# A graph network on one core: scores one tile later at the second norm, and a bias copied into PSUM in place of ten bias matmuls

## Chip, cores and metric

The kernel runs on one core of one Trainium2 chip. The metric is the device time of one execution in microseconds (us). TensorE does the matmuls, VectorE and ScalarE elementwise work and evictions of PSUM, GpSimd (POOL) set-up work and indirect DMAs, SyncE (SP) most plain DMAs.

## Reference, cut to what matters

N = 1250 nodes of D = 512 numbers, 21250 edges. Two blocks, each with a norm in front and a residual behind:

```
h = max(layernorm(x), 0)                              # first norm
hw = h @ W0 + b_w                                     # the product, with W0's bias
e = leaky_relu((hw @ a1)[dst] + (hw @ a2)[src] + b_a)
x = x + segment_sum(softmax_over_dst(e) * hw[src])
h = max(layernorm(x), 0)                              # second norm
gates = softmax(h @ gate_W + gate_b)                  # scores of 4 experts, the best 2 are taken
agg = segment_sum(h[src], dst) / degree               # neighbour sums
x = x + sum over the 2 best experts of gate * sage2(sage1(agg, h))
```

## The kernel before

Nodes are held as T = 10 tiles of P = 125 rows. Float32 products are made of three float32r matmuls each: every operand is split into a high part (a copy, made by ScalarE) and a low part (whole minus high, made by VectorE). Order between the engines is written out by hand with semaphores; each engine runs its own list in order.

**First stage, ten batches** (`tile_and_batch(b)` on TensorE, L1702 on). A batch counts edges of 125 nodes and makes the product of one tile. TensorE: turn the normed tile (4 transposes, L1716); 25 count matmuls into banks 0 to 4 (L1692), each set of five waiting for one-hots of VectorE and for the eviction of its bank; 8 matmuls of 4 columns into bank 7 (L1740, L1743), called the columns below, which wait for `hT_lo`; then the product into bank 6: a bias matmul (L1754, ones times a two-row form of the bias) and twelve matmuls (L1756 to L1758). VectorE, in each batch: loads of registers from `tab_b`, 25 one-hots (L1197), the low part of the product of the batch before (`product_low`, L1177), the low part of the turned tile (`turned_low0`, L1181). ScalarE: high part of the product (`product_high`), high part of the turned tile, five `column` instructions, the next normed row (`norm`, L756), the eviction of the five count banks (`windows_out`). Before the batches come the hot blocks (`hot_block`, L1650), with small table matmuls between them. Behind the last batch `spread` (L1700) spreads a row of source sums made by `spread_out` (L1230), which the attention weights need.

**Attention**, then the **second norm**, one loop over tiles on TensorE: `turn2` (transposes, L1828, banks 6 and 7), `neighbours1(t, 0)` (ten matmuls, L1867 and L1868, which add tile t to five neighbour sums), `logits` (8 matmuls of 8 columns, L1837 and L1838). The turned tile is evicted as high part `h2T_hi` (ScalarE) and low part `h2T_lo` (VectorE, L1389); `logits` need both. The sums of tiles 0 and 1 read `nat_a` (low part L1361), those of tile t >= 2 `nat_hi` and `nat_lo` (`rows_low`, L1378), and each the counts `CT_hi` (`counts_high`, L1356). On VectorE `attended(QN - 1)` ends the attention; behind it stand the statistics of the last two tiles, `inv_deg`, and a loop over tiles:

```python
for t in range(T):
    if t >= 2:
        rows_low(t)
    if t == 3:
        scaled(1, late)
    if t + 2 < T:
        counts_high(t + 2)
    dve.wait_ge(*h2T_hi_ready(t + 1))
    v.tensor_tensor(h2T_lo[:, :, t * P:(t + 1) * P], ...
```

The rest (two layers of four experts, then routed tiles) is not touched.

Of the kernel before, what the change touches and what calls it, by code (L numbers as in the profile page):

```python
# [14 lines left out]
F32 = mybir.dt.float32  # L15
# [22 lines left out]
def gnn_kernel(nc, x, src, dst, W0, b_w, a_vec, b_a, gate_W, gate_b, Wl, bl, Wr, out):  # L38
# [37 lines left out]
    with ctx:  # L76
# [4 lines left out]
        def at(name, shape, dt, offset):  # L81
            return nc.alloc_sbuf_tensor_at(name, shape, dt, offset=origin + offset)
# [64 lines left out]
        q_at = at("q_at", [2 * CR + 1, CR], F32, 22432)  # L147
        q_sel = at("q_sel", [2 * CR + 1, CR, P], F32R, R1 + 20480)
        a_b = at("a_b", [128, 2, D], F32, R1)
        bw_b = at("bw_b", [P, D], F32, R1 + 4096)  # L150
        spill = [at(f"spill_{k}", [128, D], F32, R1 + 6144 + 2048 * k) for k in range(2)]
        g_b = at("g_b", [NW, NCH], F32, 28704)
        g_hit = at("g_hit", [NW, NCH], F32, 29408)
# [43 lines left out]
        s_part = early("s_part", [P, T, 2], F32)  # L197
        s_both = early("s_both", [P, T, 2], F32)
        spark = early("spark", [1, 1], F32)
        bw_2 = early("bw_2", [128, D], F32R)  # L200
        ones_2 = early("ones_2", [128, P], F32R)
        column = early("column", [P, 2 * BW, G], F32)
        diag = early("diag", [P, 8, P], F32)
        assert o4[0] <= R5 + 12032
# [107 lines left out]
        def signals(names, start=0):  # L312
            return [Signal(ctx.enter_context(nc.semaphore(n)), start) for n in names.split()]
# [39 lines left out]

        (w0_hi_ready, w0_lo_ready, wa_f_ready, ab_ready, wa_ready,
         var_ready, std_ready, norm_ready, h_ready, turned, hT_hi_ready, hT_lo_ready, s_done, hw_done,
         hw_hi_ready, hw_lo_ready, bw_hi_ready, bw_lo_ready, sums_used, small_ready, s_ready, sd_ready, sd_spread, row_ready) = signals(
             "w0_hi_ready w0_lo_ready wa_f_ready ab_ready wa_ready "
             "var_ready std_ready norm_ready h_ready turned hT_hi_ready hT_lo_ready s_done hw_done "
             "hw_hi_ready hw_lo_ready bw_hi_ready bw_lo_ready sums_used small_ready s_ready sd_ready sd_spread row_ready")

        (low_ready, zl_ready, ze_ready, pf_ready, ph_ready, pl_ready, p_used, summed, den_done, rden_ready, x2_ready,
         stats_ready) = signals(
# [54 lines left out]
        def f32(ap):  # L417
            return ap.bitcast(F32)
# [145 lines left out]
        def _(pool):  # L564
# [39 lines left out]
            g.tensor_copy(wbase[:], wbase_i[:])  # L604
            g.memset(tab_x[:], 0).then_inc(consts.sem, 1)
            g.memset(tab_b[:], 0).then_inc(consts.sem, 1)
            link(g.memset(f32(bw_2[:]), 0.0))
            link(g.memset(f32(ones_2[:]), 1.0))
            pool.wait_ge(*small_in(48))
            link(g.tensor_copy(bw_2[0:1, :], bw_b[0:1, :]))  # L610
            g.tensor_tensor(bw_2[32:33, :], bw_b[0:1, :], f32(bw_2[0:1, :]), ALU.subtract).then_inc(bw_lo_ready.sem, 1)
            beyond = counts_beyond(pool)
            with pool.If(beyond):
                for q in range(QN):
# [96 lines left out]
        def _(act):  # L711
# [51 lines left out]
            def turned_high0(b):  # L763
# [2 lines left out]
                    act.wait_ge(*hw_done(b))  # L766
                copy(hT_hi[:], ps[:, 5, 0:KC * P].rearrange("p (c n) -> p c n", n=P)).then_inc(hT_hi_ready.sem, 1)

            def windows_out(b):
                act.wait_ge(*batch_done(b + 1))  # L770
                for k in range(BW):
                    copy(CT[:, :, (b * BW + k) * W:(b * BW + k + 1) * W], ps[0:P, k, 0:WT].rearrange(
                        "p (i t) -> p t i", t=T)).then_inc(window_out.sem, 1)
# [18 lines left out]
            for b in range(T):  # L792
                if b > 0:
                    product_high(b - 1)
                turned_high0(b)
                if b + 1 < T:
                    columns(b + 1)
                    norm(b + 1)
                else:
                    act.wait_ge(*spark_ready(2))  # L800
                    a.activation(spark[:], spark[:], ACT.Exp)
                windows_out(b)

            beyond = counts_beyond(act)
# [230 lines left out]
        def _(dve):  # L1035
# [328 lines left out]
            for t in range(2):  # L1364
                counts_high(t)
                first_low(t)
            attended(QN - 1)
            dve.wait_ge(*stats_ready(T))
            normed(1, late)
            dve.wait_ge(*gw_hi_ready(1))  # L1370
# [10 lines left out]
# [4 lines that stand above are left out]
                    scaled(1, late)  # L1385
                if t + 2 < T:
                    counts_high(t + 2)
                dve.wait_ge(*h2T_hi_ready(t + 1))
                v.tensor_tensor(h2T_lo[:, :, t * P:(t + 1) * P], ps[:, 6 + t % 2, 0:KC * P].rearrange(  # L1389
                    "p (c n) -> p c n", n=P), f32(h2T_hi[:, :, t * P:(t + 1) * P]), ALU.subtract  # L1390
                                ).then_inc(h2T_lo_ready.sem, 1)
            for t in range(2):
                rows_low(t)
            dve.wait_ge(*logits_done(T))
# [219 lines left out]
        def _(pe):  # L1614
# [51 lines left out]
            def sum_tables():  # L1666
                pe.wait_ge(*n_ready(1))
                pe.wait_ge(*cols_ready(1))
                mm(ps[0:NW, 7, 0:1], tri[:], tab_f[:, 1:2], start=True, stop=True).then_inc(n_summed.sem, 1)

            def turn_tables():
                pe.wait_ge(*tab_f_ready(1))
                for k in range(3):
                    last = mm(ps[0:1, 7, 4 + k * NW:4 + (k + 1) * NW], tab_f[:, k:k + 1], ident[0:NW, 0:NW], start=True,
                              stop=True)
                last.then_inc(tab_turned.sem, 1)

            for u in range(NU):
                hot_block(u)
                if u == 2:  # L1680
                    spread_spans()
                if u == 3:
                    turn_edges()
                if u == 7:
                    sum_tables()
                if u == 8:
                    turn_tables()

            def count_step(k, slot, first, opens):

# [12 lines left out]
            def tile_and_batch(b):  # L1703
                if b == 0:
                    pe.wait_ge(*tab_ready(1))
                los = first_chunks(pe, b)
                more = more_here(pe, b)

                if b > 0:
                    pe.wait_ge(*hT_lo_ready(b))  # L1710
                else:
                    pe.wait_ge(*hot_ready(len(HOT_ACT)))
                    pe.wait_ge(*hot_dve_ready(len(HOT_DVE)))
                pe.wait_ge(*h_ready(b + 1))
                for c in range(KC):
                    last = nc.tensor.transpose(ps[:, 5, c * P:(c + 1) * P], h_f[:, c * 128:(c + 1) * 128],  # L1716
                                               ident[0:P, 0:P])
                last.then_inc(turned.sem, 1)

                for k in range(BW):  # L1720

                    pe.wait_ge(*window_out(b * BW, k + 1, BW))

                    pe.wait_ge(*step_ready(b * BW, k + 1))
                    count_step(k, k, los[k], True).then_inc(step_used.sem, 1)
                with pe.If(more):
                    for k in range(BW):
                        def step(first_chunk, before):
                            pe.wait_ge(*more_ready(before, 1))
                            count_step(k, 0, first_chunk, False).then_inc(more_used.sem, 1)  # L1730
                        more_steps(pe, b * BW + k, step)

                pe.wait_ge(*hT_lo_ready(b + 1))
                if b == T - 1:
                    pe.wait_ge(*s_ready(1))
                o = ps[0:P, 7, 4 * b:4 * (b + 1)]
                if b == 0:
                    pe.wait_ge(*wa_ready(2))
                for c in range(KC):
                    first = mm(o, hT_hi[:, c], wa[:, c], start=c == 0, stop=False, skip_group_check=True)  # L1740
                    if c == 0:
                        first.then_inc(batch_done.sem, 1)
                    last = mm(o, hT_lo[:, c], wa[:, c], start=False, stop=c == KC - 1, skip_group_check=True)  # L1743
                last.then_inc(s_done.sem, 1)
                if b == T - 1:
                    spread(0)

                if b > 0:
                    pe.wait_ge(*hw_lo_ready(b))
                else:  # L1750
                    pe.wait_ge(*w0_lo_ready(1))
                    pe.wait_ge(*bw_lo_ready(1))
                o = ps[0:P, 6, :]
                mm(o, ones_2[:], bw_2[:], start=True, stop=False)  # L1754
                for c in range(KC):
                    mm(o, hT_hi[:, c], W0_hi[:, c], start=False, stop=False)  # L1756
                    mm(o, hT_hi[:, c], W0_lo[:, c], start=False, stop=False)  # L1757
                    last = mm(o, hT_lo[:, c], W0_hi[:, c], start=False, stop=c == KC - 1)  # L1758
                last.then_inc(hw_done.sem, 1)

            for b in range(T):
# [122 lines left out]
            for t in range(T):  # L1884
                pe.wait_ge(*(a_lo_ready(t + 1) if t < 2 else h2_lo_ready(t - 1)))
                pe.wait_ge(*ct_hi_ready(t + 1))
                neighbours1(t, 0)
                if t == 0:
                    pe.wait_ge(*gw_lo_ready(1))
                logits(t)  # L1890
                if t + 2 < T:
                    turn2(t + 2)
            pe.wait_ge(*h2_lo_ready(T))
            for t in range(T):
                neighbours1(t, 1)
# [181 lines left out]
```

## Time and profile before

| | |
|---|---|
| median of 3 runs | 783.39 us (781.53 to 783.49) |
| the profiled execution's own time | 783.68 us |
| its span in the trace | 781.6 us |
| mean granted clock of TensorE | 0.986 |
| TensorE busy | 750.2 us, 96% |
| VectorE, ScalarE, GpSimd busy | 395.0, 274.9, 122.8 us |

Times in the trace count from the start of the span. PE is TensorE, DVE VectorE, ACT ScalarE. Matmuls are pipelined, so one's recorded time reaches into the next; the distance from start to start is what a matmul costs in a stream. The granted clock is 1.00 at 2.4 GHz and 0.50 at 1.2 GHz.

### The profile page before, as it was taken

To read this page: it belongs to the slowest core of one execution; us is meant where nothing else is said; L and a number is where in the kernel's file an instruction comes from. 1 tells how busy PE (TensorE), PEld (TensorE's weight loads), DVE (VectorE), ACT (ScalarE), POOL (GpSimd) and SP (SyncE) were. 2 spreads that over 40 slices of the span, in tenths; PEclk is the share of its full clock that TensorE was granted. 3 is DMA by queue.
4 is the path that set the end of the run, shared out by engine and by line. 5 is a ranking of instruction groups with operands and counts; after the bars stand their busy time and mean duration, and the time that the engine had idled before them with its cause. 6 is when DMAs were issued, how large, how long until landed. Compare 5 with 4: busy or idle time off the path is not lost.

```text
span 781.6 us, 11775 instructions
## 1 busy us (share of the span) xinstructions
PE 750.2 (96%) x3755; PEld 610.1 (78%) x3755; DVE 395.0 (51%) x979; ACT 274.9 (35%) x567; POOL 122.8 (16%) x137
## 2 busy tenths in 40 slices
PE   5899999999899999999999999999999999999994
PEld 3589978888788887777777777788887888888883
DVE  8888888997652538622624424333323323323320
ACT  6945575565542521412413313111211211211221
POOL 5000000000000101840000100222322323323211
PEclk9999999999899999999999999999999999999997
DMA  9000001111401247799698781599427954339900
GB/s 219 16 4 4 3 3 34 33 33 49 147 1 55 76 132 239 220 335 341 210 366 292 244 327 60 160 271 335 86 60 193 321 173 88 67 98 262 318 12 7
DMA packets 45320, 115.10 MB, mean 147 GB/s; under 512 B 7300, under 2 KB 7432, under 8 KB 45241
## 3 DMA queue, kind: packets, MB, share of 16 engines
q1 hardware_dynamic: 28581, 77.60, 30.7%
q0 software_dynamic: 8016, 19.59, 10.8%
q10 hardware_dynamic: 8644, 16.86, 6.6%
q8 instruction: 49, 0.80, 0.4%
q14 instruction: 30, 0.25, 0.1%
HBM read 64.85 MB, written 50.07 MB: 147 GB/s over the span
## 4 chain that ended last, share of the span: by engine, by line
PE 91%; DVE 4%; ACT 2%; issue 1%; POOL 0%; DVEq 0%; ACTq 0%; POOLq 0%
PE ps L1622 18%; PE ps L1623 18%; PE ps L1624 18%; PE ps L2008 7%; PE ps L2007 6%; PE ps L1692 3%; PE ps L1867 3%; PE ps L1868 3%; PE ps L1929 2%; PE ps L2018 1%; PE ps L1973 1%; PE ps L1784 1%; PE ps L1756 1%; PE ps L1650 1%; PE ps L1758 1%; PE ps L1757 1%
## 5 line engine op out<-in xcount | busy, mean ns | idle before, releaser
L2008 PE MATMUL ps<-slots,CTs 125*128 x230 | 91.0, 396 | 0.0
L2007 PE MATMUL ps<-slots,CTs 125*128 x207 | 81.6, 394 | 0.0
L1453 DVE TENSOR_TENSOR he_t<-ps,b_b 125x512 f32<-125x512 f32 x40 | 27.5, 690 | 105.8 <-PE ps L1624 72.6
L962 ACT ACTIVATE slots<-he_t 125x512 fp32r<-125x512 f32 x40 | 25.4, 635 | 150.9 <-DVE he_t L1453 136.0
L1546 DVE CAST CTs<-ps 125x512 fp32r<-125x512 f16 (+1 forms) x69 | 37.2, 595 | 76.5 <-PE ps L1929 72.9
L678 POOL DMA_INDIRECT out<-tg,rec x23 | 37.3, 1620 | 182.2 <-ACT tg L1012 143.3
L1622 PE MATMUL ps<-W,agT_hi 128*125 128x512 f32 x160 | 63.5, 397 | 0.0
L1622 PE MATMUL ps<-W,h2T_hi 128*125 128x512 f32 x160 | 63.4, 396 | 0.0
L1624 PE MATMUL ps<-W,agT_lo 128*125 128x512 f32 x160 | 63.3, 396 | 0.0
L1623 PE MATMUL ps<-W,agT_hi 128*125 128x512 f32 x160 | 63.2, 395 | 0.0
L1623 PE MATMUL ps<-W,h2T_hi 128*125 128x512 f32 x160 | 63.2, 395 | 0.0
L1624 PE MATMUL ps<-W,h2T_lo 128*125 128x512 f32 x160 | 63.1, 394 | 0.0
L1592 DVE TENSOR_TENSOR tm<-ps,b_b 128x512 f32<-128x512 f32 x23 | 15.9, 692 | 82.0 <-PE ps L1624 82.0
L1197 DVE TENSOR_SCALAR onehot_g<-iota_h,column 125x250 bf16<-125x250 f16 x250 | 49.7, 282 | 8.3 <-PE ps L1692 7.0
L1005 ACT ACTIVATE heT<-ps 128x512 fp32r<-128x512 f32 x23 | 13.7, 598 | 107.3 <-PE ps L1973 102.9
L2008 PEld LDWEIGHTS ps<-slots,CTs 125*128 125x128 f32 x230 | 43.3, 188 | 9.6
L2007 PEld LDWEIGHTS ps<-slots,CTs 125*128 125x128 f32 x207 | 38.9, 188 | 9.0
L1622 PE MATMUL ps<-nat_hi,p_hi 125*125 125x512 f32 x100 | 42.4, 424 | 2.2 <-issue 1.8
L1016 ACT ACTIVATE agn<-ps,rec 128x512 f32<-128x512 f32 x23 | 15.8, 687 | 79.4 <-PE ps L2008 75.9
L1622 PE MATMUL ps<-slots,heT 128*128 x92 | 40.0, 435 | 0.0
L1623 PE MATMUL ps<-nat_lo,p_hi 125*125 125x512 f32 x100 | 39.6, 396 | 0.0
L1624 PE MATMUL ps<-nat_hi,p_lo 125*125 125x512 f32 x100 | 39.5, 395 | 0.0
(302 smaller groups left out, 1675.6 us busy)
## 6 DMA issues: line engine op xcount, KB each, us to landing
he_d<-slots SPq DMA_DIRECT2D x30, 448.0 KB
slots<-he_d SPq DMA_DIRECT2D x30, 448.0 KB
w_d<-slots SPq DMA_DIRECT2D x3, 4096.0 KB, 19.6
slots<-w_d SPq DMA_DIRECT2D x24, 512.0 KB
t_d<-he_t SPq DMA_DIRECT2D x40, 224.0 KB
raw<-in_L_gnn_Wl ACTq DMA_DIRECT2D x4, 1024.0 KB, 9.6
raw<-in_L_gnn_Wr ACTq DMA_DIRECT2D x4, 1024.0 KB, 5.7
slots<-in_L_gnn_Wl ACTq DMA_DIRECT2D x4, 1024.0 KB, 9.8
```

The costliest lines, as they stand in the source:

```text
L678: g.indirect_dma_start(out, bass.IndirectOffsetOnAxis(ap=i32(rec[:, i, 2:3]), axis=0), tg[i % 3][:], None, bounds_check=N - 1, oob_is_err= ...
L962: a.activation(HE[:, t, 0:D], he_t[:, (x * T + t) % 4, :], ACT.Relu).then_inc(he_hi_ready.sem, 1)
L1197: last = v.tensor_scalar(onehot_g[:, k, j, :], iota_h[:], column[:, b % 2 * BW + k, j:j + 1], None, ALU.is_equal)
L1453: v.tensor_tensor(he_t[:, n % 4, :], ps[0:P, bank_of(x, g, t), :], b1_b[:, x % 2, :], ALU.add).then_inc(pre_ready.sem, 1)
L1546: v.tensor_copy(CTs[:, 4 * r:4 * r + n, :], turned_counts(r, n)).then_inc(cts_ready.sem, 1)
L1622: mm(o, l_hi, r_hi, start=start, stop=False)
L1623: mm(o, l_hi, r_lo, start=False, stop=False)
L1624: return mm(o, l_lo, r_hi, start=False, stop=stop)
L1692: last = mm(ps[0:P, k, 0:WT], onehot_p[:, bass.ds(first + j, 1), :].rearrange("p o n -> p (o n)"), onehot_g[:, slot, j, :], start=opens an ...
L1867: mm(o, count, hi, start=t == 0, stop=False)
L2007: mm(o, CTs[:, t, :], part(k, P, t * 1024, P), start=False, stop=False)
L2008: last = mm(o, CTs[:, t, :], part(k, P, t * 1024 + D, P), start=False, stop=t == T - 1)
```

## The change

Two independent parts. At the second norm, the scores of tile t and the turning of tile t + 2 come behind the sums of tile t + 1 in place of those of tile t, and VectorE makes the low part of turned tile 0 right behind `attended(QN - 1)`. In the first stage, the bias matmul and its operands on GpSimd go; ScalarE copies the bias, held on 125 partitions, into bank 6 behind the normed row, and the twelve product matmuls add to it. One covering matmul (any data, whole bank) is put behind hot block 9.

```diff
 # gpsimd: two memsets, a copy and a subtraction that made bw_2 and ones_2 are removed
-            pool.wait_ge(*small_in(48))
-            link(g.tensor_copy(bw_2[0:1, :], bw_b[0:1, :]))
-            g.tensor_tensor(bw_2[32:33, :], ...).then_inc(bw_lo_ready.sem, 1)
 # scalar
+            def bias_in(b):
+                if b == 0:
+                    act.wait_ge(*small_in(48))
+                    act.wait_ge(*covered(1))
+                else:
+                    act.wait_ge(*hw_lo_ready(b))
+                copy(ps[0:P, 6, :], bw_b[:]).then_inc(bias_ready.sem, 1)
 # in the loop over batches, behind norm(b + 1)
+                bias_in(b)
                 windows_out(b)
 # vector
             attended(QN - 1)
+            turned_low2(0)
             dve.wait_ge(*stats_ready(T))
...
-                dve.wait_ge(*h2T_hi_ready(t + 1))
-                v.tensor_tensor(h2T_lo[...], ...).then_inc(h2T_lo_ready.sem, 1)
+                if t > 0:
+                    turned_low2(t)
 # tensor
+            def cover_product():
+                mm(ps[0:P, 6, :], q_sel[:, 0, :], q_sel[...][:, 0:D], start=True, stop=True).then_inc(covered.sem, 1)
...
+                if u == 9:
+                    cover_product()
...
-                if b > 0:
-                    pe.wait_ge(*hw_lo_ready(b))
-                else:
+                if b == 0:
                     pe.wait_ge(*w0_lo_ready(1))
-                    pe.wait_ge(*bw_lo_ready(1))
+                pe.wait_ge(*bias_ready(b + 1))
-                mm(o, ones_2[:], bw_2[:], start=True, stop=False)
...
                 neighbours1(t, 0)
-                if t == 0:
+                if t == 1:
                     pe.wait_ge(*gw_lo_ready(1))
-                logits(t)
-                if t + 2 < T:
-                    turn2(t + 2)
+                if t >= 1:
+                    logits(t - 1)
+                    if t + 1 < T:
+                        turn2(t + 1)
+            logits(T - 1)
```

## Rows read from the trace of the kernel before

**Rows 1.** The page: busy time by engine; one row of the costliest groups.

```profile
PE 750.2 (96%) x3755; PEld 610.1 (78%) x3755; DVE 395.0 (51%) x979; ACT 274.9 (35%) x567; POOL 122.8 (16%) x137
...
L962 ACT ACTIVATE slots<-he_t 125x512 fp32r<-125x512 f32 x40 | 25.4, 635 | 150.9 <-DVE he_t L1453 136.0
```

**Rows 2.** TensorE's waits, 100 us to the end: total us, times, longest.

```profile
PE ps L1837 <- DVE h2T_lo L1389: 2.9, 1, 2.9
...
PE ps L1622 <- DVE aggT L1582: 1.6, 1, 1.6
```

**Rows 3.** Timeline of TensorE, second norm: start, us, line, operation, idle before.

```profile
203.67 0.40 PE L1868 MATMUL ps<-nat_a,CT_hi 125*125 125x512 f32 x1
206.97 0.34 PE L1837 MATMUL ps<-gw,h2T_hi 128*125 128x8 f32 x1 [2.90 <-DVE h2T_lo L1389]
...
209.39 0.77 PE L1867 MATMUL ps<-nat_a,CT_hi 125*125 125x512 f32 x1
...
213.63 0.17 PE L1837 MATMUL ps<-gw,h2T_hi 128*125 128x8 f32 x1
...
214.83 0.48 PE L1867 MATMUL ps<-nat_hi,CT_hi 125*125 125x512 f32 x1
...
217.23 0.17 PE L1837 MATMUL ps<-gw,h2T_hi 128*125 128x8 f32 x1
```

**Rows 4.** Three stretches: length, busy times, then granted clock, DMA share, GB/s.

```profile
42.80:46.10 3.30, 3.21 (x8) 2.51 (x9) 3.30 (x19) 0.00 (x0) 0.00 (x0) 0.50 0.00 0
112.50:119.00 6.50, 4.30 (x18) 3.18 (x18) 6.50 (x15) 4.57 (x11) 0.00 (x0) 1.00 0.00 0
...
206.60:213.40 6.80, 6.43 (x22) 5.58 (x23) 5.08 (x10) 2.02 (x4) 0.00 (x0) 0.50 0.82 251
```

**Rows 5.** Timeline of VectorE, second norm.

```profile
200.68 0.69 DVE L1361 TENSOR_TENSOR nat_a<-h_f,nat_a 125x512 fp32r<-125x512 f32 x1 [0.87 <-ACT nat_a L715]
...
205.42 0.81 DVE L1356 CAST CT_hi<-CT 125x1250 fp32r<-125x1250 f32 x1
206.15 0.67 DVE L1389 TENSOR_TENSOR h2T_lo<-ps,h2T_hi 128x500 fp32r<-128x500 f32 x1
...
208.04 0.68 DVE L1378 TENSOR_TENSOR nat_lo<-h_f,nat_hi 125x512 fp32r<-125x512 f32 x1
```

**Rows 6.** Timeline of TensorE, products of batches 0, 2 and 3.

```profile
42.89 0.79 PE L1754 MATMUL ps<-bw,ones 128*125 128x512 f32 x1 [1.17 <-DVE W_lo L1166]
...
57.56 0.25 PE L1740 MATMUL ps<-wa,hT_hi 128*125 128x4 f32 x1
...
58.43 0.47 PE L1754 MATMUL ps<-bw,ones 128*125 128x512 f32 x1
58.74 0.39 PE L1756 MATMUL ps<-W_hi,hT_hi 128*125 128x512 f32 x1
...
65.45 0.48 PE L1754 MATMUL ps<-bw,ones 128*125 128x512 f32 x1
```

**Rows 7.** Timeline of VectorE, batches 1 to 3.

```profile
48.32 0.69 DVE L1177 TENSOR_TENSOR nat_lo<-ps,nat_hi 125x512 fp32r<-125x512 f32 x1 [0.61 <-ACT nat_hi L715]
...
55.97 0.68 DVE L1181 TENSOR_TENSOR hT_lo<-ps,hT_hi 128x500 fp32r<-128x500 f32 x1
57.51 4.97 DVE L1197 TENSOR_SCALAR onehot_g<-iota_h,column 125x250 bf16<-125x250 f16 x25 [0.86 <-PE ps L1692]
...
62.98 0.67 DVE L1181 TENSOR_TENSOR hT_lo<-ps,hT_hi 128x500 fp32r<-128x500 f32 x1
```

**Rows 8.** Timeline of ScalarE, batch 2: the normed row.

```profile
56.81 0.80 ACT L756 ACTIVATE h_f<-xs,shift,rstd 125x512 f32<-125x512 f32 x1
```

**Rows 9.** Timeline of all engines, end of the first stage.

```profile
106.73 1.27 DVE L1230 TENSOR_TENSOR diag<-ident,s_both 125x500 f32<-125x500 f32 x2 [0.65 <-DVE s_both L1224]
...
107.60 1.08 PE L1700 MATMUL ps<-diag,ones 125*125 125x500 f32 x2
...
114.32 0.47 PE L1622 MATMUL ps<-nat_hi,p_hi 125*125 125x512 f32 x1 [1.79 <-issue]
```

More of the change, by code:

```diff
@@ L149, in gnn_kernel @@
         a_b = at("a_b", [128, 2, D], F32, R1)
-        bw_b = at("bw_b", [P, D], F32, R1 + 4096)
         spill = [at(f"spill_{k}", [128, D], F32, R1 + 6144 + 2048 * k) for k in range(2)]
@@ L199, in gnn_kernel @@
         spark = early("spark", [1, 1], F32)
-        bw_2 = early("bw_2", [128, D], F32R)
-        ones_2 = early("ones_2", [128, P], F32R)
+        bw_b = early("bw_b", [P, D], F32)
         column = early("column", [P, 2 * BW, G], F32)
@@ L355, in gnn_kernel @@
          var_ready, std_ready, norm_ready, h_ready, turned, hT_hi_ready, hT_lo_ready, s_done, hw_done,
-         hw_hi_ready, hw_lo_ready, bw_hi_ready, bw_lo_ready, sums_used, small_ready, s_ready, sd_ready, sd_spread, row_ready) = signals(
+         hw_hi_ready, hw_lo_ready, bias_ready, covered, sums_used, s_ready, sd_ready, sd_spread, row_ready) = signals(
              "w0_hi_ready w0_lo_ready wa_f_ready ab_ready wa_ready "
              "var_ready std_ready norm_ready h_ready turned hT_hi_ready hT_lo_ready s_done hw_done "
-             "hw_hi_ready hw_lo_ready bw_hi_ready bw_lo_ready sums_used small_ready s_ready sd_ready sd_spread row_ready")
+             "hw_hi_ready hw_lo_ready bias_ready covered sums_used s_ready sd_ready sd_spread row_ready")
         (low_ready, zl_ready, ze_ready, pf_ready, ph_ready, pl_ready, p_used, summed, den_done, rden_ready, x2_ready,
@@ L606, in _ @@
             g.memset(tab_b[:], 0).then_inc(consts.sem, 1)
-            link(g.memset(f32(bw_2[:]), 0.0))
-            link(g.memset(f32(ones_2[:]), 1.0))
-            pool.wait_ge(*small_in(48))
-            link(g.tensor_copy(bw_2[0:1, :], bw_b[0:1, :]))
-            g.tensor_tensor(bw_2[32:33, :], bw_b[0:1, :], f32(bw_2[0:1, :]), ALU.subtract).then_inc(bw_lo_ready.sem, 1)
             beyond = counts_beyond(pool)
@@ L1366, in _, with turned_low2 @@
                 first_low(t)
+            def turned_low2(t):
+                dve.wait_ge(*h2T_hi_ready(t + 1))
+                v.tensor_tensor(h2T_lo[:, :, t * P:(t + 1) * P], ps[:, 6 + t % 2, 0:KC * P].rearrange(
+                    "p (c n) -> p c n", n=P), f32(h2T_hi[:, :, t * P:(t + 1) * P]), ALU.subtract
+                                ).then_inc(h2T_lo_ready.sem, 1)
             attended(QN - 1)
+            turned_low2(0)
             dve.wait_ge(*stats_ready(T))
@@ L1387, in _ @@
                     counts_high(t + 2)
-                dve.wait_ge(*h2T_hi_ready(t + 1))
-                v.tensor_tensor(h2T_lo[:, :, t * P:(t + 1) * P], ps[:, 6 + t % 2, 0:KC * P].rearrange(
-                    "p (c n) -> p c n", n=P), f32(h2T_hi[:, :, t * P:(t + 1) * P]), ALU.subtract
-                                ).then_inc(h2T_lo_ready.sem, 1)
+                if t > 0:
+                    turned_low2(t)
             for t in range(2):
@@ L1669, in sum_tables @@
                 mm(ps[0:NW, 7, 0:1], tri[:], tab_f[:, 1:2], start=True, stop=True).then_inc(n_summed.sem, 1)
+            def cover_product():
+                mm(ps[0:P, 6, :], q_sel[:, 0, :], q_sel[:].rearrange("p c n -> p (c n)")[:, 0:D], start=True, stop=True
+                   ).then_inc(covered.sem, 1)
             def turn_tables():
@@ L1746, in tile_and_batch @@
                     spread(0)
-                if b > 0:
-                    pe.wait_ge(*hw_lo_ready(b))
-                else:
+                if b == 0:
                     pe.wait_ge(*w0_lo_ready(1))
-                    pe.wait_ge(*bw_lo_ready(1))
+                pe.wait_ge(*bias_ready(b + 1))
                 o = ps[0:P, 6, :]
-                mm(o, ones_2[:], bw_2[:], start=True, stop=False)
                 for c in range(KC):
-                    mm(o, hT_hi[:, c], W0_hi[:, c], start=False, stop=False)
-                    mm(o, hT_hi[:, c], W0_lo[:, c], start=False, stop=False)
-                    last = mm(o, hT_lo[:, c], W0_hi[:, c], start=False, stop=c == KC - 1)
+                    mm(o, hT_hi[:, c], W0_hi[:, c], start=False, stop=False, skip_group_check=True)
+                    mm(o, hT_hi[:, c], W0_lo[:, c], start=False, stop=False, skip_group_check=True)
+                    last = mm(o, hT_lo[:, c], W0_hi[:, c], start=False, stop=c == KC - 1, skip_group_check=True)
                 last.then_inc(hw_done.sem, 1)
```

## Prediction

> **What bounds the kernel now.** I read the page first: TensorE is busy 750.2 of 781.6 us [rows 1], so a part of the change pays only where it shortens TensorE's own stream or a wait of it. Then the list of TensorE's waits behind the first 100 us: it is short, and its longest is 2.9 us, for `h2T_lo` at the scores of the second norm [rows 2]. Then TensorE's timeline there, with the granted clock. The sums of tile 0 end at about 203.9; the scores of tile 0 start at 206.97; everything from there to 213.4 runs at a granted clock of 0.50 (1.2 of 2.4 GHz) and then at 1.00 again [rows 3, 4]. The same work shows both levels: scores and turning of one tile took 2.42 us (206.97 to 209.39) and then 1.20 (213.63 to 214.83), ten sums took 4.24 and then 2.40 [rows 3]. Last, the ten batches of the first stage, engine by engine. A batch lasts 7.02 us on TensorE (58.43 to 65.45) and 7.01 on VectorE (55.97 to 62.98) [rows 6, 7]: two engines with the same period, neither much ahead of the other.
>
> **The second norm.** Nothing is added there; the order of work on TensorE and VectorE changes.
> VectorE first. Today the low part of turned tile 0 starts at 206.15, behind the last statistics and their scales, the means' divisors and a count copy (205.42) [rows 5]. The new place is right behind `attended`, so it runs at about 204.2 to 204.9 and what stood ahead of it slides by its 0.6 us of queue time. From 206.7 on the sequence is the old one: `rows_low(2)` still starts at 208.04 and ends at 208.72 [rows 5]. At the new place it waits for the high part, with all of that queued behind it; ScalarE has written the high part by then, so the wait is empty.
> TensorE next. Sums of tile 1 follow those of tile 0 at once: their low part of `nat_a` was written at 201.37 [rows 5], their counts earlier still. So 203.9 + 2.4 = 206.3. Scores and turning (tile 0, tile 2) take 1.2 at full clock: 207.5. Then the sums of tile 2 wait for `rows_low(2)`, 208.72, and start at 208.8. So the wait of some 3.07 us (203.9 to 206.97) becomes one of 1.3, now for `nat_lo`, which is late next. Behind it on TensorE stand all later sums. Today those sums start at 214.83 [rows 3], with the scores of tile 1 and the turning of tile 3 already done; these 1.20 us are still owed. Gain: 214.83 - 208.8 - 1.20 = 4.8 us. Split: 1.8 from the wait, 3.06 from the clock (6.66 us between 206.97 and 213.63 against 2.40 + 1.20 = 3.60).
> Later tiles: VectorE needs per tile one count copy, one low part of rows and one of a turned tile, 0.81 + 0.68 + 0.67 [rows 5] = 2.2 us of a tile's 3.6 on TensorE, so no wait returns. At the end the scores of tile 9 come after those of tile 8; the turned tile has then ten sums (2.40 us) and the scores of tile 8 to be evicted in by ScalarE and then VectorE, 0.67 us there [rows 5]. No DMA is issued by a moved step, and neither SP's nor POOL's queue is passed.
> The 1.3 us left over could be shorter, down to 0.6 if VectorE reaches `rows_low` sooner than it does now, or longer by the 0.6 slid, so 4.2 to 5.5 at full clock.
>
> **The first stage.** Removed on TensorE: ten bias matmuls. A slot is 0.31 us (58.43 to 58.74) [rows 6]; the product's first matmul will then follow the small column matmuls and take such a slot itself, so 0.24 (a tenth of 2.40 [rows 3]) to 0.31 is saved. TensorE's batch would fall to some 6.75 us. VectorE's stays at 7.01: one-hots, two low parts, and a gap of 0.86 us before each batch [rows 7] which follows the loads of registers of the batch, not a count (batch after batch it is 1.54 us from the start of the low part to the first one-hot, 55.97 to 57.51). So TensorE uses up the 0.91 us by which the low part (55.97 + 0.68 = 56.65) is ahead of the columns that need it (57.56) [rows 6, 7], in about four batches, and then waits 0.24 in each. What remains is VectorE's own chain. It waits for TensorE once, 0.61 us at 48.32, for the eviction of the first product [rows 7]. That product runs at clock 0.50 [rows 4] and has one matmul less (0.24 to 0.43), so VectorE moves by 0.3, at most 0.61. At the end the spreading matmul starts at 107.60; its operand is ready after the first of two `diag` instructions, 106.73 + 0.64 = 107.37 [rows 9]. So another 0.15, at most 0.23. Sum 0.45 us, bounds 0 and 0.84. What TensorE saves behind that is lost: it then idles 1.79 us for the first weights [rows 9], which VectorE and ScalarE make.
> Added: a bias copy on ScalarE in each batch, behind the normed row. No row shows ScalarE writing to PSUM. The nearest: 0.64 us for 512 wide out of and into SBUF [rows 1], 0.80 with scale and bias from columns [rows 8]. I take 0.64, being the same plain form. The normed row ends at 57.61 [rows 8], the low part it must wait for ends about when the next one starts (55.97) [rows 7], so the bias stands at 58.25 to 58.41; TensorE wants it at 58.43 [rows 6]. Free, with 0.02 to 0.18 us to spare, and later TensorE waits 0.24 for VectorE anyway. The Trainium skill, "ScalarE: Activation LUTs", "Step-by-step: what each stage is for", says that ScalarE writes PSUM faster than SBUF; no run here shows that yet, and by it the copy would be under 0.64. Queued behind the copy are the five window evictions, and TensorE's next counts wait for those; they start some 0.4 us later than now, near 58.3, and TensorE is in its twelve product matmuls until 58.74 + 12 x 0.24 = 61.6 before it comes to counts. Hidden.
> Added once: one covering matmul, at most 0.43. It stands where VectorE's chain decides: TensorE still waits 1.17 us before the first product at 42.89 [rows 6], so it costs nothing; without that cover 0.43. The GpSimd instructions removed have no waiter but that product.
>
> **Sum.** The profiled execution took 783.68 us, 781.6 of it span; the median of the runs is 783.39, 0.29 less, which is inside their spread. 783.68 - 4.8 - 0.45 = 778.4.
>
> **Rivals.** *The clock falls again in the second norm* (0.26). The wait left is 1.3 us, and 1.2 us of eight-column scores and a turning stand before it. For: after 2.9 us of idling it fell to 0.50 here [rows 3, 4]. Against: 1.79 us of idling at 112.5 to 114.3 left it at 1.00 [rows 4, 9]. A fall of half today's length costs half of 3.06, so 780.0. [...]
> *The clock falls at the start of the weighted sums* (0.08), where the idling grows from 1.79 to about 2.0: up to 1.5, so 779.8. Both falls (0.04): 781.5.
> *The first stage is TensorE's after all* (0.06): ten times 0.24 to 0.31, 2.7 in place of 0.45, 776.1. Against it stands VectorE's 7.01.
> *The gain is given back* (0.05), because later a transfer and not TensorE sets the pace: 783.4. Against: behind the second norm TensorE's longest wait is 1.6 us, for VectorE and not for a DMA [rows 2].
> *The other side: the bias copy holds up every batch* (0.03). ScalarE's copy stands between two low parts and the product. To end over 2.35 us slower it must eat 5.25 + 2.35 = 7.6 us, 0.85 in each of nine batches, on top of 0.18 and 0.24 to spare: a copy of 1.9 us, three times the nearest row. 786 or more.
>
> **Chances and range.** 778.4 itself has 0.48. Below 781.0, which is 0.3% (2.35 us, about what can be told from no change) under the median, lie it, the first two falls taken singly and the full first stage: 0.88. Both falls and the gain given back: 0.09. Slower: 0.03. The range reaches from 776.8 (wait and first stage at their good ends: 783.68 - 5.5 - 0.84 = 777.3, and a little towards the full first stage) to 781.2 (clock falls once, first stage gives nothing, wait at its bad end: 783.68 - 4.2 + 1.5 = 781.0).
>
> **What would show it.** Right: sums of tile 1 directly behind tile 0, a wait near 1.3 us before the sums of tile 2 with `nat_lo` as releaser, clock 1.00 through the second norm, batches still near 7.0 us with TensorE waiting for `hT_lo` in the later ones, first weighted sums about 0.45 us earlier. Wrong: a granted clock of 0.50 behind the new wait; batches of 6.75 us; a wait of TensorE for the bias copy; a new wait for `h2T_lo` in later tiles.

## The result, and the profile after

The changed kernel took 776.82 us (median of 5 runs, 775.18 to 777.36), the kernel before 782.69 us (5 runs, 781.16 to 783.49): ratio 0.9919 [0.9906, 0.9933]. It is faster, by more than was predicted: 778.4 was the forecast, and the median lies 0.02 us above the lower end of the range. The profiled execution took 777.36 us, 775.3 of it span, at a mean granted clock of 0.990.

The page: busy time by engine, beside [rows 1].

```profile
PE 745.5 (96%) x3746; PEld 605.7 (78%) x3746; DVE 395.0 (51%) x979; ACT 278.9 (36%) x577; POOL 120.3 (16%) x133
```

TensorE has nine instructions fewer (ten bias matmuls gone, one cover matmul added) and 4.7 us less of busy time; ScalarE has ten copies more and 4.0 us.

TensorE's waits from 100 us to the end (lines chosen): engine, line and what it waited for, then total us, times, longest.

```profile
PE ps L1629 <- issue: 2.0, 1, 2.0
PE ps L1629 <- DVE aggT L1589: 1.6, 1, 1.6
PE ps L1878 <- DVE nat_lo L1387: 0.9, 1, 0.9
```

The wait of 2.9 us for `h2T_lo` [rows 2] is gone. In its place stands one of 0.9 for `nat_lo`.

Timeline of TensorE: batches 1 to 3, the start of the weighted sums, the second norm (start, us, line, operation, idle before).

```profile
42.92 0.50 PE L1767 MATMUL ps<-W_hi,hT_hi 128*125 128x512 f32 x1 [1.16 <-DVE W_lo L1168]
...
52.73 0.59 PE L1730 MATMUL ps<-ident,h_f 125*128 125x125 f32 x4
...
56.55 0.25 PE L1757 MATMUL ps<-wa,hT_lo 128*125 128x4 f32 x1
56.66 0.47 PE L1767 MATMUL ps<-W_hi,hT_hi 128*125 128x512 f32 x1
...
59.52 0.59 PE L1730 MATMUL ps<-ident,h_f 125*128 125x125 f32 x4
...
111.06 0.47 PE L1629 MATMUL ps<-nat_hi,p_hi 125*125 125x512 f32 x1 [2.03 <-issue]
...
200.66 0.42 PE L1878 MATMUL ps<-nat_a,CT_hi 125*125 125x512 f32 x1
...
203.03 0.17 PE L1848 MATMUL ps<-gw,h2T_hi 128*125 128x8 f32 x1
203.82 0.65 PE L1839 MATMUL ps<-ident,h_f 125*128 125x125 f32 x4
205.40 0.50 PE L1878 MATMUL ps<-nat_hi,CT_hi 125*125 125x512 f32 x1 [0.94 <-DVE nat_lo L1387]
...
236.21 0.47 PE L1878 MATMUL ps<-nat_hi,CT_hi 125*125 125x512 f32 x1
```

A batch now lasts 6.79 us on TensorE (52.73 to 59.52), against 7.02 before [rows 6], and no matmul in it waits: the product follows the last column matmul by 0.11. The weighted sums start at 111.06 instead of 114.32 [rows 9]. In the second norm the sums of tile 1 start at 200.66, directly behind those of tile 0; the scores of tile 0 follow at 203.03, and the sums of tile 2 start at 205.40. The last line is the first sum of the second half (`neighbours1(t, 1)`); before, it started at 242.74.

VectorE in batches 2 and 3 and in the second norm; then ScalarE in batches 2 and 3.

```profile
54.33 0.66 DVE L1183 TENSOR_TENSOR hT_lo<-ps,hT_hi 128x500 fp32r<-128x500 f32 x1
55.73 4.97 DVE L1199 TENSOR_SCALAR onehot_g<-iota_h,column 125x250 bf16<-125x250 f16 x25 [0.75 <-PE ps L1706]
61.21 0.67 DVE L1183 TENSOR_TENSOR hT_lo<-ps,hT_hi 128x500 fp32r<-128x500 f32 x1
62.53 4.97 DVE L1199 TENSOR_SCALAR onehot_g<-iota_h,column 125x250 bf16<-125x250 f16 x25 [0.65 <-PE ps L1706]
...
200.95 0.66 DVE L1371 TENSOR_TENSOR h2T_lo<-ps,h2T_hi 128x500 fp32r<-128x500 f32 x1
...
204.67 0.68 DVE L1387 TENSOR_TENSOR nat_lo<-h_f,nat_hi 125x512 fp32r<-125x512 f32 x1
```

```profile
53.42 0.58 ACT L708 ACTIVATE hT_hi<-ps 128x500 fp32r<-128x500 f32 x1
55.05 0.80 ACT L749 ACTIVATE h_f<-xs,shift,rstd 125x512 f32<-125x512 f32 x1
55.75 0.58 ACT L708 ACTIVATE ps<-bw_b 125x512 f32<-125x512 f32 x1
60.22 0.58 ACT L708 ACTIVATE hT_hi<-ps 128x500 fp32r<-128x500 f32 x1
```

VectorE's batch shrank with TensorE's, to 6.80 (55.73 to 62.53). Its gap in front of the one-hots was to stay at 0.86; it is 0.75 and then 0.65. The bias copy took 0.58 us and ended at 56.33, 0.33 before the product.

Two stretches of the trace (length, busy times, then granted clock, DMA share, GB/s):

```profile
42.50:45.90 3.40, 2.98 (x13) 2.39 (x14) 3.40 (x17) 0.00 (x0) 0.00 (x0) 1.00 0.00 0
...
206.40:209.70 3.30, 3.30 (x11) 2.60 (x10) 1.81 (x5) 0.81 (x1) 0.00 (x0) 0.50 0.72 184
```

The clock did fall in the second norm, as a rival had it, but for half as long as before. It did not fall at the first product, where the kernel before had 0.50 [rows 4].

**Where the 6.3 us came from**, by these marks: 3.26 up to the weighted sums (114.32 to 111.06), 3.29 in the second norm (from the end of tile 0's sums to the second half: 203.90 to 242.74 is 38.84, now 200.66 to 236.21 is 35.55), and 0.2 lost among the routed tiles. The first is seven times its forecast; the second was forecast at 4.8.

### The profile page after: what moved, and what is told of

Its sections match the earlier page's. It is cut to its first block, busy times and chain, and to the rows that moved or that the text cites. A ratio compares the mean times of both kernels' runs of the same rounds, so it can differ in the third digit from the quotient of the medians.

```text
span 775.3 us, 11763 instructions
## 1 busy us (share of the span) xinstructions
PE 745.5 (96%) x3746; PEld 605.7 (78%) x3746; DVE 395.0 (51%) x979; ACT 278.9 (36%) x577; POOL 120.3 (16%) x133
## 4 chain that ended last, share of the span: by engine, by line
PE 91%; DVE 5%; ACT 2%; issue 1%; POOL 0%; DVEq 0%; ACTq 0%; POOLq 0%
PE ps L1629 18%; PE ps L1630 18%; PE ps L1631 18%; PE ps L2021 7%; PE ps L2020 6%; PE ps L1706 3%; PE ps L1878 3%; PE ps L1879 3%; PE ps L1942 2%; PE ps L2031 1%; PE ps L1986 1%; PE ps L1795 1%; PE ps L1767 1%; PE ps L1657 1%; PE ps L1769 1%; PE ps L1768 1%
```

## The experiments

Two questions. Who sets the pace of a batch: VectorE by its loads of registers, as the prediction had it, or TensorE, with VectorE following? And how much of each difference is the clock, which fell in different places in the two profiles? The ratios are to the kernel before, timed beside each kernel. The marks of the profiles, us of the span:

| kernel | start of batch 1 | start of batch 9 | weighted sums | end of tile 0's sums | second half | span | granted clock at 0.50 from |
|---|---|---|---|---|---|---|---|
| before | 47.49 | 103.67 | 114.32 | 203.90 | 242.74 | 781.6 | 42.8, 206.6, 503.6 |
| after | 45.80 | 100.28 | 111.06 | 200.66 | 236.21 | 775.3 | 206.3, 496.5 |
| bias_only | 45.81 | 100.29 | 111.05 | 201.51 | 240.40 | 779.4 | 112.1, 204.3, 501.3 |
| norm_only | 45.99 | 102.17 | 112.82 | 202.41 | 236.40 | 773.8 | nowhere |
| extra_vector_1 | 45.79 | 100.87 | 112.24 | 202.73 | 236.70 | 774.1 | 113.4 |
| extra_vector_2 | 45.79 | 104.56 | 116.39 | 205.97 | 239.95 | 778.0 | 501.0 |
| extra_scalar | 45.79 | 102.10 | 112.75 | 202.36 | 237.90 | 775.2 | 208.0 |
| rows_early | 45.79 | 100.28 | 111.06 | 200.68 | 233.46 | 770.8 | nowhere |
| rows_early_again | 45.80 | 100.31 | 111.08 | 200.71 | 233.49 | 770.9 | nowhere |
| rows_early_no_bias | 46.02 | 102.23 | 112.89 | 202.46 | 235.24 | 772.5 | nowhere |
| whole_again | 45.80 | 100.27 | 111.04 | 201.51 | 235.50 | 772.3 | 112.5 |

A batch starts with its transposes. The half clock that every profile shows over its last 7 to 9 us is left out.

**bias_only: the first stage's part alone.** VectorE's and TensorE's order in the second norm as before (parts of the edit, against the changed kernel).

```diff
-            turned_low2(0)
...
-                if t >= 1:
-                    logits(t - 1)
-                    if t + 1 < T:
-                        turn2(t + 1)
+                logits(t)
+                if t + 2 < T:
+                    turn2(t + 2)
...
```

> The bias part alone on the kernel before; the second norm as before. Theory A (TensorE paces the batches, VectorE's register loads begin when the high part of the turned tile is signalled, so they move with TensorE): batches of 6.79 us from start to start of the transposes, so 9 x 0.23 = 2.1 us less than the kernel before, 0.27%, give or take one fall of the clock at the first product (1.5 us). Theory B, the prediction's (VectorE's own batch of 7.01 us is the limit): batches stay at 7.01, at most 0.45 us less. The second norm shows its 2.9 us wait for h2T_lo again in both.

Measured: 780.34 us (778.12 to 781.27, 6 runs; before 782.66), ratio 0.9961 [0.9946, 0.9976]. The batches are those of the whole change, 6.79 us (45.81 to 100.29 is eight of them, the first 0.14 longer), as theory A had it; theory B had 7.01.

**norm_only: the second norm's part alone.** The bias matmul and its two-row operand as before, without the bias copy (parts of the edit, against the changed kernel).

```diff
...
-                pe.wait_ge(*bias_ready(b + 1))
+                if b > 0:
+                    pe.wait_ge(*hw_lo_ready(b))
...
+                mm(o, ones_2[:], bw_2[:], start=True, stop=False)
```

> The second norm's part alone on the kernel before; ten bias matmuls as before. Both theories: batches of 7.02 us; the wait of 2.9 us becomes 0.9 us for nat_lo. 4.8 us less than before if the clock stays at 1.00 behind it, 3.3 us less if it falls to 0.50 once. Together with the bias part alone it should add up to the whole change (5.9 us by the medians).

Measured: 775.78 us (775.36 to 777.25, 5 runs; before 782.66), ratio 0.9913 [0.9900, 0.9926]. Its timeline of TensorE, and two stretches with the granted clock:

```profile
112.82 0.47 PE L1627 MATMUL ps<-nat_hi,p_hi 125*125 125x512 f32 x1 [1.79 <-issue]
...
207.16 0.50 PE L1872 MATMUL ps<-nat_hi,CT_hi 125*125 125x512 f32 x1 [0.95 <-DVE nat_lo L1385]
...
236.40 0.47 PE L1872 MATMUL ps<-nat_hi,CT_hi 125*125 125x512 f32 x1
```

```profile
42.80:46.10 3.30, 3.21 (x14) 2.58 (x15) 3.30 (x19) 0.00 (x0) 0.00 (x0) 1.00 0.00 0
204.50:212.00 7.50, 6.55 (x41) 5.56 (x41) 5.79 (x11) 2.96 (x6) 0.00 (x0) 1.00 0.83 253
```

Its first stage is the old one, and its batches last 7.02. Yet its weighted sums start 1.50 us earlier than in the kernel before: the clock stayed up at the first product with the same matmuls. So 1.5 of the 3.26 us is a fall that the profile of before had and this one had not, with or without the bias part. From norm_only to after, neither with a fall ahead of the sums, the bias part is worth 112.82 - 111.06 = 1.76 us. And the second norm without a fall takes 236.40 - 202.41 = 33.99: 4.85 less than before. Against after, with its fall, that prices the fall at 1.56.

The medians of the two parts (2.3 and 6.9 us) add up to 9.2 where the whole change gives 5.9: each kernel's falls come where they come, and the marks are what adds up. By the times alone the bias part does not show on top of norm_only: its ratio, 0.9913, cannot be told from 0.9919 of the whole change. The 1.76 us is read from the marks.

**extra_vector_1 and extra_vector_2: is VectorE the pace?** One or two more VectorE instructions of 0.6 us in each batch of the changed kernel from batch 1 on, ahead of the low part of the turned tile; they write scratch that nobody reads (the edit with two).

```diff
+                if b > 0:
+                    for n in (0, 4):
+                        v.tensor_tensor(diag[:, n:n + 4, :]..., xs[:, 0, 0:4 * P], xs[:, 1, 0:4 * P], ALU.add)
                 turned_low0(b)
```

> The whole change, with one more VectorE instruction of some 0.6 us (500 wide, into scratch) in batches 1 to 9, between the low part of the product and that of the turned tile. Theory A: VectorE has about 0.65 us of idle time per batch, so batches stay near 6.8 us and the time is that of the whole change within 0.5 us. Theory B: VectorE's own batch is the limit, so each batch grows by 0.6 and the time by about 5 us.

> The whole change with two more VectorE instructions of 0.6 us in batches 1 to 9. Theory A (VectorE has about 0.7 us to spare in a batch of 6.79 us, which one instruction did not use up): with 1.2 us VectorE becomes the limit, 4.9 + 4 x 0.6 = 7.3 us a batch, about 0.45 us more in each of the later batches and some 3 to 4 us more in all. If register loads and waits add to VectorE's work as theory B said, 7.9 us a batch and 8 us more.

Measured: with one, 776.10 us (775.65 to 779.1, 6 runs; before 782.66), ratio 0.9928 [0.9911, 0.9945]. With two, 780.80 us (779.72 to 782.22, 12 runs; before 782.02), ratio 0.9991 [0.9976, 1.0005]. Timelines of the first: transposes of batches 7 to 9 on TensorE, then batch 2 on ScalarE and VectorE.

```profile
87.28 0.59 PE L1734 MATMUL ps<-ident,h_f 125*128 125x125 f32 x4
94.08 0.59 PE L1734 MATMUL ps<-ident,h_f 125*128 125x125 f32 x4
100.87 0.59 PE L1734 MATMUL ps<-ident,h_f 125*128 125x125 f32 x4
...
54.01 0.58 ACT L708 ACTIVATE hT_hi<-ps 128x500 fp32r<-128x500 f32 x1
...
54.90 0.67 DVE L1209 TENSOR_TENSOR diag<-xs 125x500 f32<-125x500 f32 x1
55.48 0.68 DVE L1183 TENSOR_TENSOR hT_lo<-ps,hT_hi 128x500 fp32r<-128x500 f32 x1
56.32 4.97 DVE L1199 TENSOR_SCALAR onehot_g<-iota_h,column 125x250 bf16<-125x250 f16 x25 [0.17 <-issue]
```

The batches stay at 6.80 and 6.79 with 0.6 us more work on VectorE, which theory B put at 0.6 us a batch. The 0.6 shows once at the start (batch 1 is 7.53 long) and once at the end, where `spread` follows VectorE. What gave way is the gap: 0.17 in place of 0.75. With two, VectorE has no gap left:

```profile
78.96 4.95 DVE L1199 TENSOR_SCALAR onehot_g<-iota_h,column 125x250 bf16<-125x250 f16 x25
83.84 0.67 DVE L1179 TENSOR_TENSOR nat_lo<-ps,nat_hi 125x512 fp32r<-125x512 f32 x1
84.44 1.25 DVE L1209 TENSOR_TENSOR diag<-xs 125x500 f32<-125x500 f32 x2
85.61 0.66 DVE L1183 TENSOR_TENSOR hT_lo<-ps,hT_hi 128x500 fp32r<-128x500 f32 x1
86.20 4.95 DVE L1199 TENSOR_SCALAR onehot_g<-iota_h,column 125x250 bf16<-125x250 f16 x25
```

Here VectorE sets the pace: 7.24 us from one-hots to one-hots (78.96 to 86.20), with 1.17 of it the added pair. Its own batch is thus 7.24 - 1.17 = 6.07 us, not 7.01, and the weighted sums start 5.3 us later than in after. Only here does TensorE wait for `hT_lo`, 2.3 us in eight batches.

**extra_scalar: how much room the bias copy has.** A copy of 125x500 in front of the bias copy in batches 1 to 8 of the changed kernel.

```diff
+                if 0 < b < T - 1:
+                    copy(diag[:, 0:4, :]..., xs[:, 0, 0:4 * P])
                 bias_in(b)
```

> The whole change with one more ScalarE copy (500 wide, into scratch, 0.6 us) between the normed row and the bias copy in batches 1 to 8. The bias stands about 0.3 us before the product wants it, so TensorE should wait 0.2 to 0.3 us for it in each of eight batches: batches of about 7.05 us, 2 to 2.4 us more. If ScalarE is not near the path, as the free copy was argued to show, batches of 6.79 us and the same time.

Measured: 776.80 us (775.29 to 779.49, 6 runs; before 782.02), ratio 0.9936 [0.9916, 0.9957]. TensorE and then ScalarE in batch 2:

```profile
56.64 0.25 PE L1759 MATMUL ps<-wa,hT_lo 128*125 128x4 f32 x1
56.98 0.49 PE L1769 MATMUL ps<-W_hi,hT_hi 128*125 128x512 f32 x1
...
55.84 0.60 ACT L708 ACTIVATE diag<-xs 125x500 f32<-125x500 f32 x1
56.35 0.58 ACT L708 ACTIVATE ps<-bw_b 125x512 f32<-125x512 f32 x1
```

The bias stands at 56.93 and the product starts at 56.98, 0.34 behind the last column matmul instead of 0.11. The batches last 7.04: what the removed bias matmul gave is taken back in full by a copy that ends 0.6 us later. The room was the 0.33 us seen above. The time, 776.80, does not show this, as the falls differ; the start of batch 9 does, 102.10 against 100.28.

**rows_early: take the rest of the second norm's wait.** `rows_low(2)` moved ahead of `turned_low2(1)`, directly behind the third counts.

```diff
-                if t >= 2:
+                if t >= 3:
                     rows_low(t)
...
                     counts_high(t + 2)
+                if t == 0:
+                    rows_low(2)
```

> The whole change, with VectorE's low part of rows of tile 2 moved ahead of the count copy of tile 3 and the low part of turned tile 1. It was ready at 205.3 us of its trace and should be near 204.0, so the wait of 0.94 us goes: 1.2 us less than the whole change. If the clock then stays at 1.00 another 1.5 us less (2.7 in all); if the scores and turnings alone let it fall, 1.2 us and no more. Rival: the count copy of tile 3 or the turned tile 1, now later, make TensorE wait instead: no gain.

Measured: 772.97 us (772.27 to 773.49, 4 runs; before 782.66), ratio 0.9875 [0.9861, 0.9889]. Once more as rows_early_again, the same kernel on another chip:

> The version with the rows of tile 2 early once more, beside the next kernel. Expected 772 to 773.5 us; batches of 6.79 us, no wait of TensorE in the second norm, its length (first sums' end to the second half's start) 32.8 us. At the start of the weighted sums TensorE idles 2.0 us, and the clock may or may not fall there (0.85 us).

Measured: 773.07 us (772.19 to 773.78, 5 runs; before 783.18), ratio 0.9879 [0.9860, 0.9898]. TensorE and VectorE of the first:

```profile
203.04 0.17 PE L1850 MATMUL ps<-gw,h2T_hi 128*125 128x8 f32 x1
203.84 0.65 PE L1841 MATMUL ps<-ident,h_f 125*128 125x125 f32 x4
204.24 0.48 PE L1880 MATMUL ps<-nat_hi,CT_hi 125*125 125x512 f32 x1
...
202.66 0.81 DVE L1358 CAST CT_hi<-CT 125x1250 fp32r<-125x1250 f32 x1
203.38 0.69 DVE L1387 TENSOR_TENSOR nat_lo<-h_f,nat_hi 125x512 fp32r<-125x512 f32 x1
```

`nat_lo` stands at 204.07 and the sums of tile 2 start at 204.24 without a wait. The second norm takes 32.78 us, 1.21 less than norm_only's 33.99, and the clock stays up in both. No version measured clearly faster: it is 9.7 and 10.1 us under the kernel before.

**rows_early_no_bias: the same edit on norm_only**, so that the bias part is priced once more, without a fall on either side. The diff is that of rows_early.

> The second norm's part with the rows of tile 2 early, ten bias matmuls as before. Against the same with the bias part (773.0): batches of 7.02 in place of 6.79, so 1.9 us more, 774.9, if falls of the clock are equal. If the bias part's longer idle time at the start of the weighted sums (2.0 against 1.8 us) lets the clock fall there, part of the 1.9 is given back and the two come within 1 us.

Measured: 775.89 us (774.55 to 777.14, 6 runs; before 782.02), ratio 0.9925 [0.9908, 0.9943]. Batches of 7.03; weighted sums at 112.89; second norm 32.78, span 772.5. Against rows_early that is 1.83 us at the weighted sums and 1.7 of the span, with no fall in either profile: the price from norm_only again. The times differ by more, 0.9925 against 0.9875 and 0.9879 of the kernel before; how much of that is falls in runs without a profile is not shown.

**whole_again: the changed kernel once more**, with no edit.

> The whole change once more, beside the kernels of this call. What the clock does is not the kernel's alone: each of four places (first product, start of the weighted sums, second norm, first routed tile) may or may not show a fall to 0.50, each worth 1 to 1.7 us. Expected: batches of 6.79 us and a second norm of 34.0 us without a fall or 35.6 us with one, from the first sums' end to the second half's start; 775 to 777.5 us. If the first figure of the change (5.9 us by the medians) were the kernel's own and not that of falls, this repeats 776.8 and the two parts alone (2.3 and 6.9) do not add up; by falls, it comes out between 774 and 777.

Measured: 775.21 us (774.09 to 776.43, 6 runs; before 782.02), ratio 0.9917 [0.9900, 0.9934]. The clock fell elsewhere this time, at the start of the weighted sums and not in the second norm (stretch with granted clock):

```profile
112.60:115.90 3.30, 3.30 (x10) 2.50 (x9) 3.30 (x8) 2.08 (x5) 0.00 (x0) 0.50 0.00 0
```

Weighted sums at 111.04, end of tile 0's sums at 201.51, second half at 235.50. So that fall costs 0.85 (201.51 against 200.66 in after, from the same start), and the second norm without a fall takes 33.99 again.

**filled: does idle time make the clock fall?** On rows_early, matmuls whose results nobody reads fill TensorE's idle time ahead of the first product and of the weighted sums.

```diff
                 if b == 0:
+                    pe.wait_ge(*w0_hi_ready(1))
+                    for _ in range(4):
+                        mm(ps[0:P, 7, 64:512], hT_hi[:, 0], W0_hi[:, 0, 0:448], start=True, stop=True, ...)
                     pe.wait_ge(*w0_lo_ready(1))
...
             pe.wait_ge(*window_out(NW))
+            for _ in range(7):
+                mm(ps[0:P, 0, :], hT_hi[:, 0], W0_hi[:, 0], start=True, stop=True, ...)
```

> The same with idle matmuls that nobody reads: four ahead of the first product (where TensorE waits 1.2 us) and seven ahead of the weighted sums (where it waits 2.0 us). If idling is what lets the clock fall at those two places, no profile shows 0.50 there and the median is up to 0.8 us lower than without, the fastest executions alike. If the fillers get in the way (they end later than the operands they wait with), the start of the weighted sums moves later by what they overrun, under 0.3 us.

Measured: 773.63 us (772.01 to 774.1, 5 runs; before 783.18), ratio 0.9882 [0.9862, 0.9902]. The idle time ahead of the sums went from 2.03 to 0.35, and they start at 111.20. The four matmuls ahead of the first product got in the way: batch 1 starts at 46.13, 0.34 later. The median was to be up to 0.8 us lower than that of rows_early_again; it is 0.6 higher, inside the spread of the runs. The clock fell nowhere, but neither did it in the two profiles of rows_early, so the question stays open.

## Why the prediction was right and where it was wrong

**Second norm: right at full clock.** 4.8 us was forecast at full clock; norm_only and whole_again show 38.84 - 33.99 = 4.85. The order came out as written: sums of tile 1 directly behind tile 0, `nat_lo` next to be late, no wait in the later tiles. The wait left was put at 1.3 and costs 1.18: the sums of tile 2 follow the start of the transposes by 1.58 (203.82 to 205.40), and by 0.40 in rows_early, where nothing waits. The rival of a second fall, given 0.26, came true in two of the six profiles with this order and this wait (after and extra_scalar; not norm_only, whole_again and the two of extra_vector). Its price was put at half of 3.06; it was 1.56. The Trainium skill, "TensorE: Matmul & The Clock Gate", "HAM oscillation — how this bites in real kernels", tells of a matmul kernel whose bursts each start at half rate behind waits for DMAs that are longer than the 0.94 us here. No run here tests that; the fall at 206.3 and norm_only's 1.00 behind the same wait are no case of it.

**Bias copy: right.** It was taken at 0.64 with 0.02 to 0.18 us to spare; it took 0.58 (573 to 580 ns, ten times) and had 0.33, less than one copy's length, as extra_scalar shows. The Trainium skill, "ScalarE: Activation LUTs", "Step-by-step: what each stage is for", has ScalarE write PSUM faster than SBUF: 0.58 against 0.635 into SBUF [rows 1] agrees, and in extra_scalar the copy into SBUF took 0.60, being 12 columns narrower. The cover matmul cost nothing: the first product starts at 42.92, before at 42.89 [rows 6].

**First stage: wrong.** The failed step is "VectorE's stays at 7.01 ... and a gap of 0.86 us before each batch which follows the loads of registers of the batch, not a count". From it came "What remains is VectorE's own chain", a wait of TensorE for `hT_lo` that the changed kernel does not have, and 0.45 us. VectorE's own batch is 6.07 us and TensorE sets the pace, so the bias part gave 1.76 to 1.83: 0.19 at the first product (45.99 to 45.80), 1.70 in the eight batches (56.18 to 54.48), less 0.13 by the end of the stage, where `spread` and the first weights still follow VectorE and ScalarE. The rival "the first stage is TensorE's after all" described it, with a chance of 0.06, and its 2.7 counted the gain in all ten batches and up to the end.

Why the gap looked fixed: VectorE's next one-hots come a fixed time after ScalarE's `hT_hi`, not after VectorE's own low part. In the kernel before, on ScalarE:

```profile
55.19 0.58 ACT L715 ACTIVATE hT_hi<-ps 128x500 fp32r<-128x500 f32 x1
```

It ends at 55.77, and the one-hots start at 57.51 [rows 7]: 1.74 later. In after, 54.00 to 55.73 and 60.80 to 62.53: 1.73 both times. In extra_vector_1, 54.59 to 56.32: 1.73, with the low part 0.89 us after the end of `hT_hi`. From the start of the low part, which the prediction took as the anchor, the same distance is 1.54, 1.40, 1.32 and 0.84. The trace has the loads themselves, in the queue of VectorE behind the low part (before, then extra_vector_1; duration in ns, then start in us):

```profile
L379 DVEq TENSOR_LOAD <-tab_b x1: 305/305/305, 56.3 to 56.3; - x1
...
L377 DVEq TENSOR_LOAD <-tab_b x1: 304/304/304, 55.1 to 55.1; - x1
L1188 DVEq TENSOR_LOAD <-tab_b x1: 299/299/299, 55.5 to 55.5; - x1
```

In extra_vector_1 the first load starts at 55.14, before the low part ahead of it (55.48). In both it starts 0.54 us behind the end of `hT_hi`, and the one-hots start 1.19 behind that. So the prediction was right that the gap follows the loads of registers; what it had wrong is when they begin. They begin when the low part's wait for `hT_hi` is met. `hT_hi` follows TensorE's transposes, so the gap moves with TensorE; VectorE had the same period because it followed. Two rivals keep the same distance: the one-hots also need ScalarE's `column` and TensorE's counts of the batch before (the releaser that the row names). But from the first load to the one-hots the instructions of VectorE's queue follow each other within 0.05 us, with no room for a wait.

**The sum.** 783.68 - 1.77 (bias part) - 1.5 (no fall at the first product) - 3.29 (second norm with a fall) + 0.2 = 777.3, against 777.36 measured. The forecast's two terms without the clock would have been 4.85 + 1.77 = 6.6, 777.1. The missing 1.3 us lies in the first stage. That the forecast missed the profiled time by no more than this is luck: the fall that did not come at the first product (1.5) and the new one in the second norm (1.56), neither of them in the main forecast, cancel. The rest is which falls a run has: 1.5 at the first product, 0.85 at the weighted sums, 1.56 in the second norm, and some 1.5 in the routed tiles (286.4 us from their start to the end in the kernel before, 285.0 in norm_only). The prediction took the 0.50 at the first product as given; whether it comes is owed to neither kernel.

## What to carry to other kernels

Two engines with the same period don't show which of them leads: look, from batch to batch and between kernels, for the event to which a gap keeps a constant distance, and price the other engine's own batch by its busy rows (here 6.07 of 7.01) before calling a gap its own. One extra instruction of known length on the suspected engine settles it: a pace that does not move belongs to another. Where the granted clock falls now here and now there, take what each part is worth from marks of its own stage in profiles with and without the fall, since medians of parts don't add up.

## What the runs showed of the hardware

VectorE's loads of registers start before the instruction ahead of them in VectorE's queue runs, once the event that it waits for has come: in extra_vector_1 0.54 us behind the event, while that instruction ran 0.89 us behind it. The first instruction after the loads came 1.73 us behind the event there, as in after. A gap before such a batch is hidden by work that is put behind the event: 0.75 us became 0.17.

The clock fell to 0.50 behind idle times of TensorE as short as 0.94 us (from 206.3 in after, 0.9 us after TensorE had gone on; scores of 8 columns and four transposes stood before the wait), and not behind the same wait in norm_only. Behind 1.17 us ahead of the first product it fell in the kernel before, and not in norm_only with the same matmuls. At the start of the weighted sums it fell in three of the eight profiles with the bias part (filled left aside), and in none of the three without it. The idle time there is 2.03 in after and 1.79 in the kernel before and in norm_only; whether the longer idle time is the reason stays open.
